# A two-layer graph attention kernel: second-layer weights in halves, values awaited by block, one eviction, two statistics steps and one GpSimd addition moved

## The reference

```python
# layers 1 and 2
xl   = (x @ W).reshape(B, N, H, F)
e    = leaky_relu(asrc[:, :, None, :] + adst[:, None, :, :], 0.2)
attn = softmax(where(mask, e, -1e9), axis=1)        # over the sources
out  = einsum('bsdh,bshf->bdhf', attn, xl)
h    = elu(layer1 + b1);  h = layer2(h) + b2
x    = layernorm(x + h)
# layer 3
Wh   = x @ W;  e = leaky(s_i[:, :, None] + s_j[:, None, :])
att  = softmax(where(adj > 0, e, -9e15), axis=1)
x    = layernorm(x + leaky(att @ Wh))
```

## Time and profile before

| | us |
|---|---|
| median of three runs | 938.67 (938.52 to 939.26) |
| profiled execution | 939.34 |
| its span | 937.1 |
| PE busy | 874.0 (93%) |
| PE weight loads busy | 815.5 (87%) |
| DVE busy | 753.4 (80%) |
| ACT busy | 687.4 (73%) |
| POOL busy | 258.1 (28%) |

### The profile page before, as it was taken

How to read it: one execution, slowest core, us unless ns; L and a number is a source line. 1 busy time by engine, 2 the same in 40 slices (tenths; PEclk the granted TensorE clock), 3 DMA queues, 4 the chain that set the end, 5 groups by cost and what they waited for, 6 DMA issues and landing times.

```text
span 937.1 us, 17310 instructions
## 1 busy us (share of the span) xinstructions
PE 874.0 (93%) x6220; PEld 815.5 (87%) x6220; DVE 753.4 (80%) x1908; ACT 687.4 (73%) x1274; POOL 258.1 (28%) x244
## 2 busy tenths in 40 slices
PE   6779889999999999999999999999999999999887
PEld 4778889998989989899998989999898998989775
DVE  6876788888788888878888887888888788887666
ACT  2686769687786877778687777868788686887653
POOL 1001020133242312434231243323224332332512
PEclk9898999999999999999999999999999999999999
DMA  7032030303013040300303021030301101000002
GB/s 217 25 106 76 1 90 2 90 2 111 3 33 81 3 111 2 85 30 25 89 1 113 2 48 65 23 92 1 114 1 46 68 23 23 1 24 1 24 1 68
DMA packets 62747, 45.03 MB, mean 48 GB/s; under 512 B 35780, under 2 KB 54340, under 8 KB 62664
## 3 DMA queue, kind: packets, MB, share of 16 engines
q1 hardware_dynamic: 62664, 43.93, 16.5%
HBM read 27.14 MB, written 8.39 MB: 38 GB/s over the span
## 4 chain that ended last, share of the span: by engine, by line
PE 38%; DVE 30%; ACT 23%; issue 9%; POOL 0%; DMA 0%; DVEq 0%; SPq 0%; POOLq 0%; ACTq 0%
DVE junk L942 9%; PE bUU L510 8%; PE bUU L531 7%; PE bG L603 6%; PE bG L621 6%; ACT att L734 5%; ACT att L749 5%; ACT x L761 4%; DVE y_lo L979 3%; PE bB L470 3%; DVE low L955 3%; DVE y L967 3%; DVE att L993 2%; ACT att L753 2%; DVE stats L1032 2%
## 5 line engine op out<-in xcount | busy, mean ns | idle before, releaser
L510 PE MATMUL bUU<-val,att 128*128 128x129 f32 x2048 | 249.2, 275 | 0.3 <-DVE att L993 0.3
L942 DVE CUSTOM_DVE_ANT_0 junk<-mask_t,bA,val 128x512 bf16<-128x512 bf16 x320 | 219.9, 743 | 33.9 <-PE bA L470 30.1
L510 PEld LDWEIGHTS bUU<-val,att 128*128 128x128 f32 x2048 | 241.4, 192 | 2.3 <-issue 0.5
L993 DVE SCALAR_TENSOR_TENSOR att<-mask_n,att 128x2048 f32<-128x2048 bf16 x78 | 178.8, 2292 | 79.3 <-ACT att L749 79.1
L734 ACT ACTIVATE att<-bB,val 128x512 f32<-128x512 f32 x320 | 202.7, 708 | 5.4 <-PE bB L470 5.4
L749 ACT ACTIVATE att<-att 128x2048 f32<-128x2048 f32 x78 | 151.5, 1942 | 0.6
L521 PE MATMUL bUU<-val,att 128*128 128x257 f32 x480 | 109.8, 381 | 1.9 <-DVE att L989 1.2
L531 PE MATMUL bUU<-val3s,att 128*128 128x256 f32 x480 | 109.2, 381 | 1.7 <-DVE res L1023 0.2
L381 POOL TENSOR_SCALAR var_eps<-moments 128x4 f32<-128x4 f32 x29 | 5.7, 195 | 368.1 <-DVE moments L1035 368.1
L802 ACT COPY val<-bG 128x524 f32<-128x524 f32 x62 | 37.6, 606 | 93.3 <-PE bG L621 93.3
L761 ACT ACTIVATE x<-bUU,zinv 128x128 f32<-128x128 f32 x256 | 73.4, 375 | 43.8 <-DVE zinv L973 43.8
(11 more groups left out here) (126 smaller groups left out, 1635.8 us busy)
## 6 DMA issues: line engine op xcount, KB each, us to landing
adj_in<-in_adj_dram SPq DMA_DIRECT2D x16, 1024.0 KB, 5.8
x_in<-in_x_dram SPq DMA_DIRECT2D x16, 512.0 KB, 6.7
out_dram<-act SPq DMA_DIRECT2D x14, 512.0 KB, 2.9
mask_t<-mask_n SPq DMA_TRANSPOSE x64, 2.5
att<-in_L_gnn_W_dram SPq DMA_DIRECT2D x4, 128.0 KB, 3.1
val<-in_L_gnn_W_dram SPq DMA_DIRECT2D x1, 512.0 KB, 7.2
out_dram<-x_in SPq DMA_DIRECT2D x1, 512.0 KB, 2.9
w<-in_L_gnn_W_dram SPq DMA_DIRECT2D x1, 256.0 KB, 7.4
```

The source lines that it names most:

```text
L510: ins = nc.tensor.matmul(to[:, (d % 2) * FX:(d % 2 + 1) * FX], p[:, s, d * P:(d + 1) * P], val1[u.batch % 2][:, s, u.index // 2, values], ...
L942: nc.vector.tensor_tensor_reduce(junk[:, b] if u.row else att[u.slot % 3][:, b], mask_t[u.batch % 4][:, b], bA[:], 1.0, a_col(u, b) if u.r ...
L993: nc.vector.scalar_tensor_tensor(flat(p), mask_n[u.batch % 3][:, 0:NB * N], BIG, flat(p), ALU.add, ALU.min)\
```

## The change

Six edits, each in the order or the waiting of work that was there before:

1. Every L2 unit is made in halves, as `halved_second` was. A running count `u.p` of pieces takes the place of `u.r` in the waits.
2. `attend_3`, part 0, first target block: the wait for all four blocks of `val3s` becomes a wait for block j ahead of its matmul.
3. ACT, pos 5: `values_1_out(n+1, 2)` moves ahead of the second half of `leaky`, right behind `normalize`.
4. DVE: `norm_stats` of `res2` moves from the end of pos 4 to pos 5, behind `invert`.
5. DVE, pos 1: `second_out(…, 2)` moves behind `tops` and `shifted_targets` of the next unit.
6. POOL, pos 3: `add_bias_2(n-1)` waits until `b_t` of head h3 of batch n is ready. The two calls after the loop, for the last batch, have no such wait.

```diff
+    pieces = 0
     for u in units.values():
         u.h = H * u.batch + u.index
+        u.p = pieces
+        if u.row:
+            pieces += 1 if u.kind == "h" else NB if u is final_second else 2
...
                 if pos == 3 and 0 <= n - 1 < B:
+                    pool.wait_ge(b_t_ready, units[SLOTS * n + H].r + 1)
                     add_bias_2(n - 1)
...
             def attend_2(u, i):
-                pe.wait_ge(prob_done, u.r + 1 + (i if u is halved_second else 0))
+                pe.wait_ge(prob_done, u.p + i + 1)
...
             def attend_3(u, i):
-                pe.wait_ge(val3s_done, (u.batch + 1) * NB)
                 for d in range(2):
                     for j in range(NB):
+                        if i == 0 and d == 0:
+                            pe.wait_ge(val3s_done, u.batch * NB + j + 1)
...
             def exps(u, blocks=range(NB)):
-                if u is halved_second:
+                if u.kind == "L2":
...
                     normalize(older)
+                if pos == 5 and batch:
+                    values_1_out(n + 1, 2)
                 if this:
                     leaky(this, (2, 3))
...
-                if pos == 5 and batch:
-                    values_1_out(n + 1, 2)
                 if this:
                     exps(this)
...
             def keep_edges(u):
-                if u is halved_second:
+                if u.kind == "L2":
...
                     invert(older)
+                if pos == 5 and 0 <= n - 3 < B:
+                    norm_stats(n - 3, 1, res2, res2_done, 2, stats2, moments2)
...
-                if pos == 1 and units.get(g - 2):
-                    second_out(units[g - 2], 2)
                 if last_head:
                     low_part(last_head)
                 if after:
@@
                     shifted_targets(after)
                 if pos == 0 and units.get(g - 1):
                     second_out(units[g - 1], 0)
+                if pos == 1 and units.get(g - 2):
+                    second_out(units[g - 2], 2)
...
-                if pos == 4 and 0 <= n - 3 < B:
-                    norm_stats(n - 3, 1, res2, res2_done, 2, stats2, moments2)
```

More of the change, by code:

```diff
@@ L64, in gat_kernel @@
     final_head, final_second = units[SLOTS * END + H], units[SLOTS * (END + 1) + 5]
-    halved_second = units[LAST - 1]
     PARTS = (range(0, 2), range(2, 3), range(3, 4))
@@ L506, in attend_head @@
                 to = u_bank(u.use[i])
-                pe.wait_ge(prob_done, u.r + 1)
+                pe.wait_ge(prob_done, u.p + 1)
                 for d in range(2 * i, 2 * i + 2):
@@ L538, in attend_2_by_sources @@
                 for s in sources:
-                    pe.wait_ge(prob_done, u.r + s + 2)
+                    pe.wait_ge(prob_done, u.p + s + 1)
                     for d in range(NB):
@@ L984, in keep_edges @@
                 dve.wait_ge(diag_done, u.batch + 1)
-                if u is halved_second:
+                if u.kind == "L2":
                     mask = mask_n[u.batch % 3][:, 0:NB * N].rearrange("p (b n) -> p b n", n=N)
                     for i, half in enumerate((slice(0, N // 2), slice(N // 2, N))):
-                        dve.wait_ge(exp_done, u.r + i + 1)
+                        dve.wait_ge(exp_done, u.p + i + 1)
                         nc.vector.scalar_tensor_tensor(p[:, :, half], mask[:, :, half], BIG, p[:, :, half], ALU.add, ALU.min)\
@@ L991, in keep_edges @@
                     return
-                dve.wait_ge(exp_done, u.r + 1)
+                dve.wait_ge(exp_done, u.p + 1)
                 nc.vector.scalar_tensor_tensor(flat(p), mask_n[u.batch % 3][:, 0:NB * N], BIG, flat(p), ALU.add, ALU.min)\
@@ L1201, in _ @@
                     x_low(n + 1)
-                if this is halved_second:
+                if g == LAST - 1:
                     invert(final_head)
@@ L1224, in _ @@
                 p = att[final_second.slot % 3]
-                dve.wait_ge(exp_done, final_second.r + s + 2)
+                dve.wait_ge(exp_done, final_second.p + s + 1)
                 nc.vector.scalar_tensor_tensor(p[:, s], mask_n[END % 3][:, s * N:(s + 1) * N], BIG, p[:, s], ALU.add, ALU.min)\
```

## The result

The changed kernel takes 906.92 us (median of four runs, 906.74 to 909.11), against 938.6 us for the kernel before beside it. The ratio is 0.9667 (95% interval 0.965 to 0.9683). The forecast was 908.5 with a range of 903.5 to 917; the measured gain is 31.7 us. The profiled execution took 906.74 us, its span is 904.8 us; before these were 939.34 and 937.1, so the profiled gain to explain is 32.6 us.

The account below looks back on a forecast made before the run. PE was taken as the bound, gains coming only where it stands idle; 5.6 + 11.5 + 3.7 + 7.5 + 0.4 + 1.6 + 0.2 = 30.5 off 939.34 or 938.67 gave 908.5 us, range 903.5 to 917.

Parts of the forecast that it names:

- the four places: Idle weight loads at pos 3 (0.62 us), pos 5 (0.96), pos 0/1 (0.34) and pos 1 (0.68), together 2.60 of 55.20.
- guard on POOL: Pos 3: the addition no longer holds `low`; 0.62 less 0.15 for a new gap, 12 times, 5.6 us.
- pos 5, statistics and copy: Pos 5: `normalize` and the copy of block 2 come earlier, the idle 0.96 us goes, 12 times, 11.5 us.
- `val3s`: by block and halves: Ahead of `attend_3`: waiting by block and an earlier chain close 0.34 us, 11 times, 3.7; halves gain 0.
- residuals: Pos 1: residuals behind the maxima let `b_t` come 1.0 us earlier, closing 0.68, 11 times, 7.5 us.
- Either edit alone would free most: Pos 5: moving only the statistics or only the copy would free most of the 0.96 us.
- Start and end: Outside the periods: start gains 1.6 us (0 to 3), end 0.2 (0 to 1.9).
- the 0.4 "in the period before": Pos 1: 0.4 us gained from one gap of 0.4 in the period before the eleven gaps of 0.68.
- rivals 1 and 3: 1: tight wait at pos 1 or 4 stays open, 915.7, chance 0.18; 3: late L407 holds the minimum, 929.5, chance 0.04.
- (4): Pos 3: minimum held 2.4 us and the ELU up to 2.4, slower than before, 962; chance 0.02.
- (5): Whole period: PE's idle time is no loss, another limit stands right behind, 937 to 940; chance 0.02.
- Rival 2: PE's gates fall wholly: minimum not held, start gains 3, end 1.9; 903.6, chance 0.14.

Follow-up runs that it names:

- the one-input addition: GpSimd's bias addition replaced by two one-input instructions, bias of layer 2 left out, on the kernel before: 931.99 us, ratio 0.9915.
- the version above: The changed kernel with the last batch's bias addition moved behind `scale_3(END-2)` on GpSimd: 904.91 us, ratio 0.9629.

## Why the prediction was right, and where its terms were off

The time (908.5 forecast, 906.9 measured), the bound (PE), the four places and the signs of the main terms were right, and so was the order of size. That the sum came nearer than its terms is partly luck: three terms were too small by 0.11 to 0.25 a period and the fourth too large by 0.30. What the period gave, place by place; "shown" is the loss when the step is undone in the changed kernel:

| step of the sum | forecast a period | shown |
|---|---|---|
| guard on POOL | 0.47 | 0.66 |
| pos 5, statistics and copy | 0.96 | 1.21 |
| `val3s`: by block and halves | 0.34 | 0.45 |
| residuals | 0.68 | 0.38 |
| sum | 2.45 | 2.70 |
| measured period | | 2.66 |

The losses need not add up, since one edit can close part of another's gap, so 2.70 beside 2.66 is no proof of the single rows. Of the signs that the prediction named for being right, two weren't met: the period is 52.54, below its 52.7 to 52.9, and `normalize` of pos 5 still waits for `zinv`, 0.44 where it was 1.77. One that it named for being wrong came, minima longer than 2.3 us, but without a cost in this kernel.

**Guard.** The mechanism was as told: L407 held `low`, the wait frees it, the minimum comes next behind the addition. The term mis-sized is the 0.15 for a new gap ahead of `bB` of L2. The prediction took the minimum to be held for the full 0.44; it was lengthened by 0.27 (2.56 against 2.29), with 0.41 of the addition left. And the load of `bB` stands 0.20 us behind the end of `b_t` (463.42 against 463.22) with no idle time. The new gap is 0.00. The longer minimum does have a price, but at the copy of pos 5 and only while the statistics stand ahead of it: 0.22 a period with the guard alone.

The Trainium skill (SBUF — State Buffer, "Who interferes with whom") gives the one who starts first the ports for the whole instruction. In this case that is what `low` shows behind the addition (L407 before, L411 after; two inputs, 2.36 us) and behind L409 (one input, 1.04 us): each time it ends when they do. The minimum behind the addition agrees with it only in sign (0.27 of 0.41), and minimum against L394 not at all.

**Pos 5.** The gap closed as told, but two readings failed. "Either edit alone would free most": the copy alone gives 0.41 of the 1.21 a period (53.75 to 53.34), the statistics alone all of it (the copy back costs 0.00). The prediction looked at one consumer of `normalize`'s queue, the copy; ACT's whole queue behind `normalize` is late, and PE then stands in pieces of 0.19 to 0.35. And the term of 0.96 was the gap as it stood; with the guard in place it is 1.18, by the longer minimum of pos 3 (1.18 with both edits of pos 5 undone and with the guard alone, 0.96 with the one-input addition).

**`val3s`.** The two legs named were the wait by block and the earlier chain. The halves were said to gain nothing, as cover; they are the third leg. A whole minimum of L2 ends later: `y_lo`, next on DVE, starts 4.23 us behind the start of the exponentials with whole weights and 3.44 with halves (477.28 − 473.05 with the halves undone, 475.07 − 471.63 in the changed kernel). The ELU, the reciprocal, the weights of L3 and `val3s` stand behind it on DVE and ACT. The step that failed is "nowhere the last thing that PE waits for": true in the trace of before, no longer when the other gaps are closed. Either leg alone covers most, so the sum was right with the wrong attribution.

**Residuals.** The gap of 0.68 closed, but 0.25 to 0.3 of it would have closed without this edit: the statistics alone bring it from 0.68 to 0.42. The prediction did count that DVE's chain moves by about 1.7, then gave the whole gap to the residuals. The slack it gave, 0.2, is 0.43 in the trace, without idle time at the load.

**Start and end.** The start was put at 1.6 and gave 0.71, counted from the first `bB` to unit 14 (137.81 against 137.10). The rest of the 1.9 up to unit 17 belongs to other terms: 0.5 at unit 15 is the 0.4 "in the period before", and 0.7 at unit 17 is the first `low` that the guard frees. Of the start's own parts the copy gave 0.8 (0.7 forecast) and the lengthened minimum of batch 1 cost 0.26 (half a microsecond forecast). The term that failed is the 1.0 of the residuals. At 122.61 PE waited 3.33 us; in the kernel after:

```profile
122.05 0.65 PE L476 MATMUL bB<-ident,b_t 128*128 128x128 f32 x4 [2.64 <-DVE b_t L967]
122.10 0.88 DVE L1030 SCALAR_TENSOR_TENSOR res<-bUU,z2inv,x_in 128x256 f32<-128x256 f32 x2
...
130.47 0.65 PE L476 MATMUL bB<-ident,b_t 128*128 128x128 f32 x4 [1.57 <-DVE b_t L967]
```

Of the 0.7 gained at 122, 0.4 are given back by 130.47: DVE limits in this stretch, so residuals moved behind one unit's `b_t` stand ahead of the next one's. Busy us by engine (PE, PEld, DVE, ACT, POOL), clock and DMA of the kernel before and then of after:

```profile
125.00:130.00 5.00, 5.00 (x34) 4.70 (x34) 4.56 (x16) 4.32 (x8) 1.23 (x2) 0.76 0.56 201
```

```profile
125.00:130.00 5.00, 3.73 (x30) 3.56 (x30) 5.00 (x18) 5.00 (x8) 1.23 (x2) 1.00 0.60 215
```

DVE is busy all 5 us after. PE's granted clock is 0.76 in this stretch before and 1.00 after (1.00 is 2.4 GHz; below it, part of the stretch ran at 1.2), which the prediction had as a bound only. It gave nothing here: from one `bB` to the next, around this stretch, it is 8.01 us before and 8.42 after, and 8.42 too with the halves undone, where the clock was 0.79. The end was held as told: the unguarded addition keeps `low` until 845.60, and the version above shows its price, 2.0 us, close to the bound of 1.9. Of the 1.95 us of units 72 to 79, 0.96 are the twelfth time of the gap at pos 5 (before, at 818.56). Some 0.7 more are won right behind it, where PE stood for 0.20, 0.41 and 0.20 us before and doesn't after; with the 0.3 lost behind unit 79 the end gave about 0.7 where the sum had 0.2.

None of the rivals took place. No load of `bB` of L2 waited (rivals 1 and 3), no minimum exceeded 2.57 us (4), and PE's gaps were real losses (5). Rival 2, at 903.6, was nearest in its first half: the gap behind the guard did stay closed, though the minimum was lengthened.

## What to carry to other kernels

Undo edits from the finished kernel as well as adding them to the old one: the guard was worth 0.43 us a period alone and 0.66 at the end, the copy nothing once the statistics had moved, the statistics 1.61 alone and 0.80 at the end. Where a bound engine waits at several places, look for the one instruction group ahead of an engine's whole queue (here the statistics ahead of `zinv`) before treating the places one by one; and ask of each edit what it lengthens on another engine and where the bound engine next waits behind that engine: the guard's longer minimum was paid at pos 5, two slots later, until that place was closed too. Long GpSimd instructions belong where VectorE's next short instruction is not on the way of the bound engine.

## What the runs showed of the hardware that was not expected

- A GpSimd instruction with one input (1.04 us) holds a four-column VectorE instruction until it ends, just as one with two inputs (2.36 us) does.
- A minimum of 128x2048 that begins with 0.41 us of the addition left takes 2.56 us instead of 2.29, so it loses 0.27 and not 0.41. All 15 minima that begin so take 2.56 to 2.57 us. The 0.27 cost PE nothing in the changed kernel and 0.22 a period with the guard alone.
- Minimum and L394 (GpSimd, 128x256) can lengthen each other. In the kernel with both edits at pos 5 undone the second half minimum, beside two L394, takes 1.41 us (1.22 alone), and an L394 that begins just ahead of the first half takes 2.26 (1.22 alone); in the changed kernel, where all 30 halves take 1.215 to 1.227, only L394 grows, up to 3.32.
- TensorE's granted clock dropped for short stretches in single executions, behind long waits in the start and the tail. In the kernel with the halves undone it was 0.79 in the stretch 125 to 130 us and 0.66 in 850 to 855, just behind a wait of 2 us in the tail; in the changed kernel 1.00 in both. The eight matmuls of 128x257 behind the wait in the tail took 2.56 us there and 2.00 in the changed kernel; with the copy put back, at 0.75 in 850 to 855, they took 3.04. So these two profiled times are above what the periods say. The changed kernel itself took 906.7 to 906.9 us in three executions with a mean clock of 0.989 and 909.1 in one with 0.985. Which execution gets such a stretch isn't settled by these runs.
